# A second block's own one-hot tile and PSUM bank in the attention's aggregation of a graph-network kernel

## The reference, cut to what matters

```python
xw = (x @ W).reshape(N, HEADS, D_HEAD)
e = leaky_relu(a_src[src] + a_dst[dst], 0.2)
e_max = segment_max(e, dst, num_segments=N)
e_exp = exp(e - e_max[dst])
denom = segment_sum(e_exp, dst, num_segments=N)
alpha = e_exp / (denom[dst] + 1e-16)
out = segment_sum(xw[src] * alpha[:, :, None], dst, num_segments=N)   # then + bias
# afterwards: 25 steps of a leaky integrate-and-fire count over out
```

## Time and profile before

| what | value |
|---|---|
| median of 3 runs | 8082.64 us (8075.37 to 8092.41) |
| the profiled execution's own time | 8090.67 us |
| its span | 8088.9 us |
| TensorE busy | 3395.1 us (42%) |
| VectorE busy | 3385.8 us (42%) |
| ScalarE busy | 1163.0 us (14%) |
| GpSimd busy | 5650.1 us (70%) |
| mean granted TensorE clock | 0.548 of full speed |
| the attention's pass | 2460.56 to 3121.58 us |

### The profile page before, as it was taken

The page is one execution under the profiler, slowest core; times in us unless marked ns, Lnnn a source line. Parts: engine busy times, 40 slices in busy tenths (PEclk is TensorE's granted clock), DMA queues, the critical chain, the costliest instruction groups (busy, mean ns, idle before and its releaser), DMA issues.

```text
span 8088.9 us, 81271 instructions
## 1 busy us (share of the span) xinstructions
PE 3395.1 (42%) x13888; PEld 2581.8 (32%) x13889; DVE 3385.8 (42%) x7359; ACT 1163.0 (14%) x2052; POOL 5650.1 (70%) x5838
## 2 busy tenths in 40 slices
PE   4554441000005664443555543333355545455553
PEld 3444441000005553113444421111144444344442
DVE  6446665000026557972333333333433333433335
ACT  3000003333321114760000000000100000200001
POOL 2777676777777724777777777777577777477774
PEclk6555555555556665665555555555555555555555
DMA  2222112555542331012222222222211221121211
GB/s 71 53 53 50 49 49 62 135 134 135 134 112 76 87 85 33 28 38 57 72 72 72 72 68 79 79 79 79 70 52 53 52 53 52 48 52 53 53 52 47
DMA packets 348725, 555.52 MB, mean 69 GB/s; under 512 B 121283, under 2 KB 200983, under 8 KB 348623
## 3 DMA queue, kind: packets, MB, share of 16 engines
q0 software_dynamic: 199680, 357.35, 18.3%
q1 hardware_dynamic: 148943, 197.20, 8.0%
HBM read 448.57 MB, written 105.56 MB: 69 GB/s over the span
## 4 chain that ended last, share of the span: by engine, by line
POOL 32%; issue 21%; PE 20%; DVE 15%; DMA 6%; DVEq 5%; ACT 1%; SPq 0%; ACTq 0%; POOLq 0%
POOL GATHERED L628 27%; PE PS L736 19%; POOL list_dram L641 5%; DVE OH L1306 3%; DVE OH L1300 2%; DMA GATHERED<-row_tab,SRCI 2%; DVEq L321 2%; DMA GATHERED<-typed_b_tab,PLACE 2%; DVE T L1141 1%; DVE EX L1546 1%; DVE SM L1151 1%; DVE EQ L1326 1%; DVEq L323 1%; DMA GATHERED<-gat_tab,SRCI 1%; DVE PS L1499 1%
## 5 line engine op out<-in xcount | busy, mean ns | idle before, releaser
L736 PE MATMUL PS<-GATHERED,OH 128*128 128x128 f32 (+2 forms) x9216 | 2424.8, 441 | 2860.7 <-DVE OH L1300 898.6
L628 POOL DMA_INDIRECT GATHERED<-row_tab,SRCI x2496 | 2363.1, 947 | 965.6 <-issue 677.2
L736 PEld LDWEIGHTS PS<-GATHERED,OH 128*128 128x128 f32 (+1 forms) x9216 | 1900.4, 301 | 3443.9 <-issue 1910.5
L641 POOL DMA_INDIRECT list_dram<-REC,PLACE x832 | 910.1, 1094 | 490.4 <-issue 262.2
L628 POOL DMA_INDIRECT GATHERED<-gat_tab,SRCI x832 | 785.9, 945 | 278.9 <-issue 229.8
L628 POOL DMA_INDIRECT GATHERED<-typed_b_tab,PLACE x832 | 786.8, 946 | 262.6 <-issue 219.9
L628 POOL DMA_INDIRECT GATHERED<-typed_tab,KEYF x832 | 791.8, 952 | 253.6 <-issue 239.2
L1300 DVE TENSOR_TENSOR OH<-IOTA,PS 128x512 f32 (+3 forms) x1024 | 702.8, 686 | 493.2 <-issue 471.3
L1306 DVE TENSOR_SCALAR OH<-IOTA,DSTF,WF 128x128 f32 x2048 | 580.1, 359 | 428.0 <-issue 402.9
L1323 DVE TENSOR_TENSOR T<-T,PS 128x128 f32 x512 | 147.0, 287 | 965.8 <-PE PS L736 964.6
L736 PE MATMUL PS<-T,OH 128*128 128x132 f32 x2048 | 429.5, 384 | 246.9 <-DVE OH L1300 145.4
(11 more groups left out here) (278 smaller groups left out, 3265.5 us busy)
## 6 DMA issues: line engine op xcount, KB each, us to landing
gat_rows<-GATHERED SPq DMA_DIRECT2D x208, 264.0 KB, 2.3
GATHERED<-gat_rows SPq DMA_DIRECT2D x208, 264.0 KB, 2.7
GATHERED<-row_tab,SRCI POOLq DMA_INDIRECT x2496, 2.5
ROWI<-dst_rows SPq DMA_DIRECT2D x208, 128.0 KB
typed_b_tab<-ACC SPq DMA_DIRECT2D x49, 384.0 KB, 2.4
list_dram<-REC,PLACE POOLq DMA_INDIRECT x832
GATHERED<-gat_tab,SRCI POOLq DMA_INDIRECT x832
GATHERED<-typed_tab,KEYF POOLq DMA_INDIRECT x832, 2.5
```

Of the source, the lines that this page charges most:

```text
L628: pool.indirect_dma_start(out=rows_at[:, u * CT + t, 0:width], out_offset=None, in_=table, in_offset=bass.IndirectOffsetOnAxis(ap=rows[:, ...
L641: pool.indirect_dma_start(out=list_dram, out_offset=bass.IndirectOffsetOnAxis(ap=PLACE[:, t:t + 1], axis=0), in_=REC[:, 2 * t:2 * t + 2], ...
L736: last = mm(bank(p)[:, 0:r.shape[1]], onehot(p, t, 1, onehots_), r, start=(t == 0), stop=(t == CT - 1))
```

## The change

In the walk `gb` alone, the second block gets a one-hot tile of its own (`EQ`, the size of one tile of `OH`) and a bank of its own (bank 2). VectorE's part for it, comparison, wait, addition, moves ahead of its wait for the first sums. TensorE no longer waits after the second sums until they are added. It waits ahead of them instead, for the addition of the further block before (`before + w + 1`), since the bank is shared by all further blocks. VectorE's last wait of the moved part is for its own addition of the second sums (`hold_here`).

```diff
-            def sums(rows, ready, k, p, onehots_):
+            def sums(rows, ready, k, p, onehots_, into=None):
...
-                    last = mm(bank(p)[:, 0:r.shape[1]], onehot(p, t, 1, onehots_), r, start=(t == 0), stop=(t == CT - 1))
+                    last = mm(bank(p if into is None else into)[:, 0:r.shape[1]], onehot(p, t, 1, onehots_), r, start=(t == 0), stop=(t == CT - 1))
...
                         with pe.Fori(0, more) as w:
-                            sums(lambda t: rows(u, t), wk.more_onehot, before + w, u % 2,
-                                 onehots_).then_inc(wk.more_sums, 1)
-                        hold(pe, wk.more_added, before + more + 1)
+                            if apart:
+                                hold(pe, wk.more_added, before + w + 1)
+                                sums(lambda t: rows(u, t), wk.more_onehot, before + w, 0, EQ, 2).then_inc(wk.more_sums, 1)
+                            else:
+                                sums(lambda t: rows(u, t), wk.more_onehot, before + w, u % 2,
+                                     onehots_).then_inc(wk.more_sums, 1)
+                        if not apart:
+                            hold(pe, wk.more_added, before + more + 1)
...
+                def second_blocks(c, u, more, before, first):
+
+                    with others(u % sets):
+                        with dve.Fori(0, more) as w:
+                            b = within(first + w + 1, NB)
+                            onehots(c, b, 0, weights, EQ).then_inc(wk.more_onehot, 1)
+                            hold(dve, wk.more_sums, before + w + 1)
+                            add(b, 2).then_inc(wk.more_added, 1)
+                        hold_here(dve, wk.more_added, before + more + 1)
...
+                        if apart:
+                            second_blocks(c, u, more, before, first)
                         hold(dve, wk.sums, c + (wk.turn * NCH + 1))
...
                         (add_joined(first, p) if joins else add(first, p)).then_inc(wk.added, 1)
-                        with others(u % sets):
+                        if not apart:
+                            with others(u % sets):
```

More of the change, by code:

```diff
@@ L735, in sums, with aggregate @@
                     r = rows(t)
-                    last = mm(bank(p)[:, 0:r.shape[1]], onehot(p, t, 1, onehots_), r, start=(t == 0), stop=(t == CT - 1))
+                    last = mm(bank(p if into is None else into)[:, 0:r.shape[1]], onehot(p, t, 1, onehots_), r, start=(t == 0), stop=(t == CT - 1))
                 return last
-            def aggregate(name, rows_ready, rows, table=RANGES, parts=((NIT, None, None),), sets=1, onehots_=OH):
+            def aggregate(name, rows_ready, rows, table=RANGES, parts=((NIT, None, None),), sets=1, onehots_=OH, apart=False):
                 wk = walks[name]
@@ L837, in _ @@
             aggregate("gb", lambda i, u: hold(pe, v_made, RING * i + (u + 1 + RING)),
-                      lambda u, t: VX[:, u * CT + t, :])
+                      lambda u, t: VX[:, u * CT + t, :], apart=True)
             def typed_beside(g, t):
@@ L1315, in aggregate @@
             def aggregate(name, result, F, weights=None, ahead=None, table=RANGES,
-                          parts=((NIT - 1, None, None),), sets=2, joins=False):
+                          parts=((NIT - 1, None, None),), sets=2, joins=False, apart=False):
                 wk = walks[name]
@@ L1351, in chunks @@
                         (add_joined(first, p) if joins else add(first, p)).then_inc(wk.added, 1)
-                        with others(u % sets):
[L1353 to L1361, removed]
+                        if not apart:
+                            with others(u % sets):
+                                with dve.Fori(0, more) as w:
+                                    b = within(first + w + 1, NB)
+                                    onehots(c, b, p, weights, of).then_inc(wk.more_onehot, 1)
+                                    hold(dve, wk.more_sums, before + w + 1)
+                                    if joins:
+                                        hold(dve, wk.more_added, before + w + 1)
+                                        join(p, 2).then_inc(wk.more_joined, 1)
+                                        hold(dve, wk.more_joined, before + w + 1)
+                                    (add_joined(b, 2) if joins else add(b, p)).then_inc(wk.more_added, 1)
                         dve.nop(nofuse=True).then_inc(wk.free, 1)
@@ L1727, in _ @@
             weigh(0, 0, 16)
-            aggregate("gb", lambda b: ACC[:, bass.ds(b * XW, XW)], XW, None, ahead)
+            aggregate("gb", lambda b: ACC[:, bass.ds(b * XW, XW)], XW, None, ahead, apart=True)
             DEN = SM[:, 0:NB * HEADS].rearrange("p (b h) -> p b h", h=HEADS)
```

## The result

The changed kernel takes 7955.53 us (7949.76 to 7966.14, 4 runs) beside 8086.74 for the kernel before: ratio 0.9841, interval 0.9824 to 0.9858, some 128 us less (131 between the medians). That is faster, as forecast. It is inside the range of 7955 to 8047 by half a microsecond, where the kernel's own runs spread over 16, so that it fell inside and not outside is luck. The size is 1.6 times the forecast 80 us, and past the likeliest case's own bounds (7985 to 8020). The profiled execution took 7966.14 us, the longest of the four.

What follows compares the result with a forecast made beforehand. The attention's pass, where VectorE and TensorE wait for each other, was taken to bound the kernel. Terms -89 - 10 + 14 + 5 = -80 us gave 8003 us against the median 8082.64; range 7955 to 8047.

Steps and rivals of the forecast that it cites:

- likeliest case: Whole program: the summed terms hold without any rival; 8003 us, bounds 7985 to 8020, chance 57%.
- The wait behind the second sums: Chunk behind a second block: TensorE goes straight on, so VectorE's 48 waits there vanish; 89 us gained.
- E: End of the second sums on TensorE; the next chunk's products were to start 0 to 0.7 us after it.
- the rival of a late restart: TensorE's control work waits for the last products, restart at E + 1.38; 20% together with a falling clock, 8042 us.
- The second comparison ahead of the first wait: Chunks with a second block: its 0.69 us lie beside late first sums, removing 16 waits of 0.6; 10 us gained.
- The first addition behind the second, and the added wait: VectorE between second and first addition: a new gap of 0.3 us, bounds 0.08 to 0.6, 48 times; 14 us lost.
- Branches: 160 chunks without a second block: jump moves behind a running comparison; taken at nothing, at most 32 us lost.
- ScalarE is four chunks ahead: Behind the added wait on VectorE: the next weighing is queued there, with ScalarE taken to be four chunks ahead.
- What is late next, and the clock: Second chunk behind a second block: TensorE only level with VectorE; 5 us lost, up to 16. Clock rising was a rival.
- the band of 0.6 to 0.75: TensorE's granted clock expected in the next profile's pass; leaving it would mean the prediction was wrong.
- that rival: The clock rises in the pass because TensorE's work is denser: about -120 us in all, 7963 us, chance 14%.
- Slower, or no change: VectorE's longer loop fetches code each turn, up to 8110 us, 5%; or gains cancel or don't carry, 8083 us, 4%.

Runs made afterwards that it cites:

- the restart alone: Changed kernel with VectorE back in its old order (first addition before the second block's comparison), TensorE still let off: 7992.69 us, ratio 0.9873 to the kernel before.
- the filled pauses: Kernel before, plus four unread products on TensorE behind the second sums, ahead of its wait: 8020.46 us, ratio 0.9905 to the kernel before.
- VectorE's order alone: Changed kernel with TensorE's wait after the second sums put back: 8036.28 us, ratio 0.9919 to the kernel before.
- The jump put back: Changed kernel plus a jump around an empty instruction behind the first addition: 8005.28 us, ratio 0.9886 to the kernel before.

## Why the prediction was right, and where its size was off

*The wait behind the second sums.* Right in mechanism and size: -89 forecast, -90 found. The restart came at E + 0.09, at the near end of the bound of 0 to 0.7; the rival of a late restart, which the earlier trace rows spoke against, is excluded by the row at 2576.76, by all 48 restarts (0.08 us in the mean, none over 0.52) and by the restart alone (-103 us). The prediction's parts for VectorE's way to the next addition add up to 2.84 us, not 2.7; it was there at E + 2.45, and the wait was gone either way.

*The second comparison ahead of the first wait.* -10 forecast, -12 found, but the agreement is luck in part: in the old order this wait fell to 0.01 with the restart alone and to -0.01 with the filled pauses, so 7 or 8 of the 12 us would have gone without the moved comparison.

*The first addition behind the second, and the added wait.* 0.29 us against 0.3, +14 both ways. The runs added what I had missed: this loss exists only because the restart is gone as well. In the kernel with VectorE's order alone it lies in TensorE's pause.

*Branches.* This is the term that was mis-sized: "Taken at nothing; without that cover it costs at most the gap". I looked at where the jump goes and not at where it comes from. Behind a comparison of 0.69 us it is covered, as I said; behind an addition of 0.29 us it was not, and this was visible in the gap that I used for another term, 0.28 at 2588.95. The gaps gave -33 us in the trace. The jump put back returned 24 of them and costs some 32 us with the register load (36 of the total by the ratios, with the lower clock). The other 9 us of the 33 lie around the second blocks, where the restart alone took the gap behind from 0.31 to 0.06; what made that part isn't shown. That "ScalarE is four chunks ahead" does not hold everywhere either: 26.0 us of the idle time before weighings ended with ScalarE before, and 15.2 still do.

*What is late next, and the clock.* +5 was forecast for TensorE being level in the second chunk behind, and +5 was found there. What the sum lacked was the clock: it rose to 0.89 and left the band of 0.6 to 0.75, one of the prediction's own signs of being wrong, and with it the wait for the second sums fell by 8 us and that in the other chunks by 6. I gave that rival 14% and the time 7963, which is within 8 us of the time measured, but in the main for another reason: its 39 us for the clock are 14 in the two waits, and of the 48 us beyond the forecast up to 33 are the gaps behind the additions. "Against it: at full clock TensorE works for only 1.14 us of a chunk's 2 or so" was the argument that failed. From 2580 to 2600 us of the changed kernel the granted clock was 1.00, with TensorE busy 11.67 of the 20 us. What brought most of the half clock before was the pause behind the second sums: filling that pause in the kernel before was enough for 0.91. The Trainium skill's advice to keep TensorE busy continuously ("TensorE: Matmul & The Clock Gate", section "Why this matters for your kernels") was borne out by this run in its direction, though the added work is thrown away. Continuously busy TensorE was not even so: 374 of the pass's 580 us.

*Slower, or no change.* The longer loop was not fetched each turn: VectorE's gaps at the register load stayed at 0.13 to 0.19 us, and the whole trace has 85 and 17 packets in the instruction queues, as before.

## What to carry to other kernels

When two engines take turns, look for the wait that stands between an engine and work whose inputs are ready; here a tile and a bank of their own removed it, and the gain (90 us of 661) could be read from one row of waits. Then price a moved branch at both ends: what it will lie behind, and what it lay behind. And where the granted clock is mixed, price half clock in every wait on TensorE, and try filling its pauses before the code is rearranged: on the kernel before, that alone gave 77 us, where the whole change gave 128. The two don't add up, since 40 of the 77 lie in the wait that the change removes; but two unread products on top of the change still gave 20.

## What the runs showed of the hardware that I had not expected

- A jump over code that is not run left 0.15 us of idle VectorE, in the mean, behind an addition of 0.29 us, and none behind a comparison of 0.69 us. Some 200 of them cost about 30 us, 8 of them at the register load that follows.
- 384 more matmul records in the pass (2432 in place of 2048) made it 81 us shorter, since the granted clock rose from 0.67 to 0.91.
- At full clock the next chunk's products began 0.09 us after the second sums' end (0.52 us at most in 48), although a loop's end, a wait, a register load and two branches lie between them in TensorE's program; behind a wait that held, the same stretch took 1.38 us from the end of the addition it waited for.
